# Half of a tile's normalisation computed by ScalarE instead of VectorE, in the expert stage of a vision tower on one core

## What is computed

```python
logits = xf @ router_w
gate_vals, idx = jax.lax.top_k(logits, 2)
gates = softmax(gate_vals)
for e in range(8):
    h = relu(xf @ w1[e] + b1[e]) @ w2[e] + b2[e]
    y = layernorm(xf + h) * gamma[e] + beta[e]      # (x - mu) * rsqrt(var + 1e-6), per token
    w = sum(where(idx == e, gates, 0), axis=-1)
    out = out + w[:, None] * y
```

## Time and profile before

| | us |
|---|---|
| median of 3 runs (967.09 to 975.83) | 969.73 |
| the profiled execution | 962.15 |
| its span on the core | 960.4 |
| PE busy in the span | 808.4 |
| DVE busy | 766.4 |
| ACT busy | 570.7 |
| POOL busy | 505.1 |

### The profile page before, as it was taken

One profiled execution on the slowest core, in us unless ns is written; L12 is line 12 of the kernel. 1 busy time (PEld: TensorE's weight loads), 2 busy tenths in 40 slices (PEclk: granted clock), 3 DMA queues, 4 the chain that ended last, 5 costly groups with the idle time before them and its releaser, 6 DMA issues.

```text
span 960.4 us, 27884 instructions
## 1 busy us (share of the span) xinstructions
PE 808.4 (84%) x7819; PEld 680.3 (71%) x7820; DVE 766.4 (80%) x3156; ACT 570.7 (59%) x1536; POOL 505.1 (53%) x684
## 2 busy tenths in 40 slices
PE   2799989989999999999998549999999999999600
PEld 2599989946667777777776338888898888888500
DVE  2767888536689989999998517999999999999956
ACT  2533441038699999999997126666666666666400
POOL 3000000000278888887888845777787777777700
PEclk9999999989799999999997579999999999999955
DMA  8443320080012212121212336222222222222089
GB/s 178 118 78 73 59 59 2 1 247 16 19 51 59 62 55 60 58 59 52 64 55 59 91 92 249 79 67 74 74 75 69 73 73 66 69 74 76 25 311 385
DMA packets 68202, 84.19 MB, mean 88 GB/s; under 512 B 12067, under 2 KB 52694, under 8 KB 67978
## 3 DMA queue, kind: packets, MB, share of 16 engines
q1 hardware_dynamic: 52295, 53.27, 20.2%
q0 software_dynamic: 12256, 22.50, 7.5%
q10 hardware_dynamic: 3555, 7.23, 2.2%
HBM read 48.15 MB, written 35.71 MB: 87 GB/s over the span
## 4 chain that ended last, share of the span: by engine, by line
PE 41%; DVE 25%; issue 13%; DMA 7%; ACT 4%; POOL 4%; SPq 2%; DVEq 1%; ACTq 1%; POOLq 0%
PE ps L675 8%; PE ps L775 5%; DVE arena L1368 4%; DVE arena L1043 4%; DMA arena<-y_tokens 4%; PE ps L750 3%; PE ps L761 3%; DVE arena L1389 3%; PE ps L824 3%; DVE arena L1362 3%; PE ps L756 2%; PE ps L810 2%; PE ps L829 2%; PE ps L843 2%; DMA y_tokens<-arena 2%
## 5 line engine op out<-in xcount | busy, mean ns | idle before, releaser
L586 POOL DMA_INDIRECT y_tokens<-arena x184 | 183.5, 997 | 87.5 <-DVE arena L1389 46.1
L559 POOL DMA_INDIRECT x_slots<-arena x192 | 186.8, 973 | 57.6 <-POOL arena L557 51.3
L933 PE MATMUL ps<-arena 128*128 x1472 | 180.6, 276 | 0.2 <-ACT arena L1630 0.2
L933 PEld LDWEIGHTS ps<-arena 128*128 128x128 f32 x1472 | 171.6, 192 | 1.7 <-issue 0.5
L1630 ACT ACTIVATE arena<-ps,b_t 128x256 f32<-128x256 f32 x368 | 144.6, 475 | 22.0 <-issue 12.0
L675 PE MATMUL ps<-wt,arena 128*128 128x128 f32 x960 | 118.0, 280 | 12.0 <-DVE arena L1043 12.0
L675 PEld LDWEIGHTS ps<-wt,arena 128*128 128x128 f32 x960 | 112.7, 195 | 13.4 <-DVE arena L1043 13.4
L922 PE MATMUL ps<-arena 128*128 128x256 f16 x368 | 101.3, 275 | 15.6 <-DVE arena L1337 11.6
L923 PE MATMUL ps<-arena 128*128 128x256 f16 x368 | 100.8, 274 | 0.0
L924 PE MATMUL ps<-arena 128*128 128x256 f16 x368 | 100.8, 274 | 0.0
L564 POOL MEMSET arena<- 128x258 f32 x1 | 0.3, 317 | 189.0 <-DVE arena L1293 189.0
(11 more groups left out here) (208 smaller groups left out, 1840.5 us busy)
## 6 DMA issues: line engine op xcount, KB each, us to landing
arena<-x_slots SPq DMA_DIRECT2D x92, 130.0 KB, 2.2
arena<-y_tokens SPq DMA_DIRECT2D x17, 640.0 KB, 14.3
h<-h_rows SPq DMA_DIRECT2D x1, 5440.0 KB, 17.0
out<-h ACTq DMA_DIRECT2D x17, 320.0 KB, 9.2
arena<-x_in SPq DMA_DIRECT2D x64, 84.5 KB
arena<-x_in SPq DMA_DIRECT2D x56, 78.0 KB
h_rows<-h SPq DMA_DIRECT2D x32, 128.0 KB
x_slots<-arena POOLq DMA_INDIRECT x192
```

Of the source, the lines that this page charges most:

```text
L559: pool.indirect_dma_start(xs_dram, bass.IndirectOffsetOnAxis(ap=slot_i[n][0:rows, t, k:k + 1], axis=0), row[n][0:rows, k, t, :], None).the ...
L586: pool.indirect_dma_start(y_dram, bass.IndirectOffsetOnAxis(ap=y_id[n % 2][:, k:k + 1], axis=0), y_sl[n % 2][:, k, :], None, bounds_check= ...
L933: ins = pe.matmul(ps[6 + m][:, 128 * k:128 * k + 128], hid[m][:, c, 128 * k:128 * k + 128], w2_sb[:, bass.ds(e, 1), c, :].rearrange("p o n ...
```

## The change

ACT computes the second half of the normalisation (`k = 1`), as `scale * x + bias` with `scale` = gate times 1/sqrt(variance) and `bias` = minus mean times scale. DVE keeps the first half. The bias, `nb3` (`128 x 1`), is made by DVE in `gated_rstd`, linked behind the product `rg3` that it reads. On ACT the new work stands first in an iteration, with a lag of 5. `LAST_TILE_LAG` goes from 5 to 6, so each engine's loop has one more turn. On DVE `tile_moments` moves from behind `scaled` to ahead of it. `scaled` also waits for the new semaphore `half_ready`.

```diff
-LAST_TILE_LAG = 5
+LAST_TILE_LAG = 6
...
             def sums(i, n, u, e):
...
                 need(dve, S["norm_ready"], i - 1)
+                need(dve, S["half_ready"], i - 1)
...
             def gated_rstd(i, n, u, e):
                 dve.wait_ge(S["rstd3_ready"], i + 1)
-                dve.tensor_tensor(rg3, rstd3, x_sl[n][:, :, E_DIM], ALU.mult).then_inc(S["gate_ready"], 1)
+                need(dve, S["half_ready"], i)
+                ch.link(dve.tensor_tensor(rg3, rstd3, x_sl[n][:, :, E_DIM], ALU.mult))
+                dve.scalar_tensor_tensor(nb3, mv3[:, 1, 0:1], -1.0, rg3[:, 1:2], ALU.mult, ALU.mult).then_inc(S["gate_ready"], 1)
...
             def tile_norm(i, n, u, e):
                 dve.wait_ge(S["gate_ready"], i + 1)
                 need(dve, S["scl_ready"], i)
-                for k in range(2):
-                    ins = dve.tensor_scalar(nrm[:, k, :], res[n % 2][:, k, :], mv3[:, k, 0:1], rg3[:, k:k + 1],
-                                            ALU.subtract, ALU.mult)
-                    if k == 0:
-                        ch.step(ins)
-                ins.then_inc(S["norm_ready"], 1)
+                dve.tensor_scalar(nrm[:, 0, :], res[n % 2][:, 0, :], mv3[:, 0, 0:1], rg3[:, 0:1],
+                                  ALU.subtract, ALU.mult).then_inc(S["norm_ready"], 1)
...
             def scaled(i, n, u, e):
                 dve.wait_ge(S["norm_ready"], i + 1)
+                dve.wait_ge(S["half_ready"], i + 1)
...
                 at(4, tile_norm)
                 at(3, tile_stats)
+                at(3, tile_moments)
                 at(4, scaled)
-                at(3, tile_moments)
                 at(4, shifted)
...
+            def second_norm(i, n, u, e):
+                act.wait_ge(S["gate_ready"], i + 1)
+                need(act, S["scl_ready"], i)
+                act.activation(nrm[:, 1, :], res[n % 2][:, 1, :], ACT.Identity, bias=nb3, scale=rg3[:, 1:2])\
+                   .then_inc(S["half_ready"], 1)
+
             def tile_iteration(at):
+                at(5, second_norm)
                 at(2, relu, range(FC))
                 at(0, upper_half)
                 at(4, tile_rstd)
```

More of the change, by code:

```diff
@@ L297, in build @@
         y_sl = [A3.take(2, E_DIM) for _ in range(2)]
-        bns3, mv3, ln3, rstd3, rg3 = (A3.take(2, 6), A3.take(2, 2), A3.take(2), A3.take(2), A3.take(2))
+        bns3, mv3, ln3, rstd3, rg3, nb3 = (A3.take(2, 6), A3.take(2, 2), A3.take(2), A3.take(2), A3.take(2), A3.take(1))
         y_id = [A3.take(2, dt=I32) for _ in range(2)]
@@ L319, in build @@
             "cnt_ready cnt_ps tab_f_ready tab_ps pad_first pad_ready tab_ready pad_gone pad_stored xs0 "
-            "xs1 xs2 xs3 xs4 xs5 xs6 xs7 norm_ready scl_ready gate_ready bns3_ready xt_ps xhi_ready xlo_ready "
+            "xs1 xs2 xs3 xs4 xs5 xs6 xs7 norm_ready half_ready scl_ready gate_ready bns3_ready xt_ps xhi_ready xlo_ready "
             "h_ps h_ready w2_ps xb_ready t_ready rstd3_stats rstd3_ready y_ready yg0 yg1 yl0 yl1 yl2 yl3 "
```

## The result

The changed kernel took **1029.75 us** in the median of 4 runs (1022.14 to 1032.94), the kernel before 971.24 in the 4 runs beside it (967.09 to 975.83): a ratio of 1.066 (95% interval 1.059 to 1.074). It is slower, as forecast, and by more: 58.5 us instead of the forecast's 37. The profiled execution of after took 1022.14 us at a mean granted clock of 0.937, the same as before. Over the expert stage alone the clock was 0.99 (0.97 to 1.00 in windows of 50 us) against 1.00 before, and PE waits there, so the clock does not explain the loss.

The account below looks back on a forecast made before the run. PE (3.46) and DVE (3.52 us busy of 3.68 per tile) bound the kernel; L580 holding L1389 every tile adds 0.44 over 84 tiles, with the tail +37.5: 962.15 to 999.7, plus 7.6 for the median, 1007; range 968 to 1013.

Parts of the forecast that it names:

- e + 3.14: On POOL: e is the end of L1389; after a late `y_ready` the next L580 starts 3.14 us later.
- the delay: What the change adds to DVE's way from one L1389 to the next: forecast +0.32 us per tile.
- ACT's ring: Rival: ACT's first relu, delayed by waiting for `nb3`, makes `second_layer` late and PE waits; 1005 us, chance 0.05.
- The added wait of `scaled`: On DVE: waiting for `half_ready`, raised by things done long before, costs 0, at most 0.1 us.
- the one of no change: Rival: L1389 is still held in every second tile and DVE's loss mostly hidden; 972 to 977 us, chance 0.26.
- steps 2 to 4: On DVE per tile: moments behind stats and `shifted` behind `scaled`, together +0.38 us; link and `nb3`, +0.19.
- held, L1389 ends 0.16 after L580: On DVE: L580 holds L1389 in every tile, so its end comes 4.03 us after the last; further delay makes this safer.
- the still-stand's tile: Every 8 tiles DVE stands still 1.62 us, taken as its register load; that tile was to take 4.75 us.
- such a tile takes no hit: On DVE: the tile with the 1.62 us standstill, one in 8, is not held by L580.
- the threshold: L580 starting 0.69 us after the pair L1389 holds it, 0.70 left one free; 0.70 was forecast, taken as held.
- the signs: Expected in the profile: L1389 1.5 to 1.6 us in nearly every tile, POOL's DMA idle 1.01, PE's clock still 1.00.
- PE's 3.46 as a floor: PE's busy time of 3.46 us per tile is its least, so at most 0.22 per tile can be gained.

Follow-up runs that it names:

- e4: The changed kernel without POOL's tensor_tensor L580, the second bias left out of the result: 971.92 us, ratio 1.006.
- e6: The changed kernel with a POOL memset of about L580's length in place of L580, second bias left out: 971.74 us, ratio 1.006.
- e9: The kernel before with a POOL memset of about L580's length in place of L580, second bias left out: 939.89 us, ratio 0.974.
- e3: The kernel before with the link and an added `nb3` on DVE that nobody reads: 1009.9 us, ratio 1.038.
- e2: The changed kernel with the moments back behind `scaled`, the second half kept on ACT: 980.21 us, ratio 1.012.
- e5: The kernel before without POOL's tensor_tensor L580, the second bias left out of the result: 942.74 us, ratio 0.976.
- e7: The kernel before with one line changed: POOL's L580 for the next tile waits until DVE has added the present one (`sums`): 948.1 us, ratio 0.974.
- e10: The kernel before with one DVE wait on its own `gate_ready` added behind L1362: 1075.54 us, ratio 1.051.
- e8: The changed kernel with POOL's L580 for the next tile waiting until DVE has added the present one (`sums`): 1024.48 us, ratio 1.012.
- e1: The kernel before with only the moments moved ahead of `scaled` on DVE: 1021.2 us, ratio 1.052.
- e11: The kernel before with the link and an unread `nb3` made twice on DVE, each linked: 1072.51 us, ratio 1.059.

## Why the prediction was half right

**Right.** L580 is what holds DVE (e4 to e6 and e9). The hold locks in, tile after tile between two register loads, once DVE is late enough, and POOL's start-up makes it stay: 0.86 from L1389's end to the DMA in every tile, L580 at e + 3.14 (846.58 to 849.72), both as worked out. A delay of 0.31 gave 4.03 per tile and 32.94 per group (e3), so the mechanism and its sum held at the delay that they were worked out for. The tensor_scalar gave its 0.25 back. ACT's activation was hidden, and ACT's ring did not bind. The added wait of `scaled` costs 0.03, inside the 0 to 0.1 allowed. No rival came true for the changed kernel; e2, with a delay of 0.06, comes nearest to the one of no change.

**Wrong: the size of steps 2 to 4, the delay.** This is the step that failed first. +0.32 was forecast and +0.60 came. The terms are read from one tile of after, with L1364 at 842.55 and L1337 at 842.93:

```profile
843.73 0.28 DVE L1352 BATCH_NORM_STATS2 arena<-arena 128x6 f32<-128x128 f32 x1
...
844.47 0.44 DVE L1378 TENSOR_TENSOR arena<-arena 128x256 f32<-128x256 f32 x1
844.95 0.57 DVE L1386 CAST arena<-arena 128x2 int32<-128x2 f32 x1
```


| term | forecast | measured in after |
|---|---|---|
| one tensor_scalar less | -0.25 | -0.25 |
| second stats to `scaled` | 0.42 + 0.16 | 844.47 - 843.73 = 0.74 |
| `scaled` to the copy | 0.48 | 844.95 - 844.47 = 0.48 |
| together, less the old 0.68 | +0.38 | +0.54 |
| link and `nb3` | +0.19 | 842.93 - 842.55 - 0.07 = +0.31 |

I took the idle of the earlier trace rows, 0.15, and 0.16 for two moments that had stood close together behind long work. They are 0.19 of idle (0.46 to 0.47 from the stats) and 0.28 from the first moment to `scaled` (848.48 to 848.76): with no long work ahead of them, the short instructions took longer from start to start. Likewise `nb3` was costed by what it "holds" (0.07), though L1337 begins 0.19 after it starts (847.02 and 847.21). From `scaled` to the copy it was 0.48 in this tile and 0.58 in the one shown first (848.76 and 849.34); both occur.

**Wrong: the sum's "held, L1389 ends 0.16 after L580", and with it 4.03 for any larger delay.** The sum took it that further delay only makes the hold safer; from 0.41 on the tile is longer, 4.23 to 4.28. With the delay of 0.60 L1389 would have started at e + 2.72. The copy L1386 ahead of it took 0.46 instead of 0.17, to within 0.1 of the end of POOL's second DMA (849.72), and L1389 started at e + 3.13, together with L580. Neither half of the pair was through, so both came behind it: its end is 0.43 after L580's (850.87 and 850.44) where it had been 0.16, and 0.27 is about one half of the pair. 3.14 + 0.72 + 0.43 = 4.29. That the DMA holds the copy is read from the two ends. e4 bears it out: without L580 the copy is long too (760.22, 0.36 us) and ends with the DMA, at 760.58. But `shifted` starts all the same 0.14 behind the copy's start there (760.36) and takes 0.61. So the DMA alone does not make L1389 late; that it starts with L580 is seen only where L580 is there, and why is not shown.

**Wrong: the still-stand's tile.** In this group it came to 5.23 instead of 4.75 (35.19 less 7 x 4.28), in others with nothing else to disturb them to between 4.72 and 5.23. That "such a tile takes no hit" was misread, too: in the kernel before, L1378 of the tile of the earlier trace rows takes 0.63 (859.30) instead of 0.40 beside L580 (859.60). All together: 35.19 - 32.96 = 2.23 us per group, of which 7 x 0.25 = 1.75 is the longer tile. That is 0.28 per tile, x 84 = 23, which is the distance from 1007 to 1029.75.

**Wrong: the threshold read as a distance.** The tile of 622.79, free at 0.70, is not a lone case: e3 has such a tile in nearly every group, at 0.68 to 0.70, and holds the others at the same distance. It did not matter for the changed kernel, whose L1389 starts with L580. Of the signs, L1389 took 1.15 and not 1.5 to 1.6, POOL's idle was 1.28 and not 1.01, and the clock was not 1.00 throughout.

**Wrong: PE's 3.46 as a floor.** The busy time of matmuls overstated it; start to start it is 3.31, and 3.37 over a whole group (e5). **The Trainium skill**, "Trainium Kernel Development and Optimization", section "Performance Expectations", calls matmul busy time a bad metric for how close a kernel is to roofline, since matmuls are pipelined, and e5 agrees. It made no difference for the changed kernel, but it hid what was to be had: 3.67 against 3.37 is 0.30 per tile, and one line (e7) got 0.22 of it.

## What to carry to other kernels

When two engines hold each other up, look at the phase in which they meet before the length of either's list: here one line that fixes the phase was worth 2.6%, and two swapped lines with the same work cost 5%. A short instruction between long ones cost 0.07 to 0.09 here from its start to the next, and 0.18 to 0.20 when the next waited for it, so "moved" work that had filled a wait is not free. Take the floor of a pipelined engine from start to start of the same instruction in a stretch in which it waits for nothing, not from its busy time.

## What was not expected of the hardware

- A wait on a semaphore that the engine's own instruction, just issued, is to raise left DVE idle for 0.32 to 0.33 us behind the 128x2 L1362 (e10), but for 0.19 behind a 128x128 stats (after).
- An indirect DMA on POOL starts 0.16 to 0.17 us after the instruction before it when its semaphore is there (e7, e8), and 0.85 to 0.86 after the releasing instruction's end when it is not (e3, after). That start-up is more than L580 itself (0.72).
- A POOL DMA and DVE's work lengthened each other in either direction: the DMA 1.18 to 1.19 instead of 0.98 (e1, e10, e11) and up to 1.25 with no L580 in the kernel (e5), or the copy 0.46 to 0.57 instead of 0.17 (after). The cause is read from the times alone.
- A tensor_tensor and a memset on POOL of 0.72 and 0.67 us differ by 58 us in a kernel of 1030 (after, e6). The memset held no `shifted`, but it did hold the tensor_scalar L1373, 0.88 instead of 0.34.
- The same pair was held or went free with L580 at the same distance, 0.69, behind its start (e3: 843.20 and 867.39).
